# Attention with the next image's projections woven into the current image, keys times tokens instead of keys times values, and a mix phase that works in pairs

## What is computed

```
q, k, v = split(x @ W_qkv.T)                 # 8 heads of 32 channels
q = sigmoid(q);  k = sigmoid(k);  v = v / (scale * c // H)
sink_incoming   = 1 / (((q + EPS) * (k_sum + EPS)).sum(-1) + EPS)
source_outgoing = 1 / (((k + EPS) * (q_sum + EPS)).sum(-1) + EPS)
conserved_sink   = ((q + EPS) * ((k * source_outgoing).sum(2) + EPS)).sum(-1) + EPS
conserved_source = ((k + EPS) * ((q * sink_incoming).sum(2) + EPS)).sum(-1) + EPS
kv = einsum('bhnd,bhne->bhde', k, v * softmax(clip(conserved_source)) * n)
x_update = einsum('bhnd,bhde->bhne', q, kv) * sink_incoming * sigmoid(conserved_sink)
out = x_update @ W_proj.T + b_proj
```

## Time and profile before

| | |
|---|---|
| time, median of 3 runs | 5708.57 us (5692.53 to 5710.28) |
| the profiled execution | 5696.53 us, its span 5694.8 us |
| PE busy | 5394.3 us, 95% of the span |
| DVE, ACT, POOL busy | 3966.5, 2635.7, 2496.2 us |
| mix phase | from 2960 to 4055 us |
| attention phase | from 4055 to 5237 us |
| mean granted clock of TensorE over the execution | 0.973 of 2.4 GHz |

### The profile page before, as it was taken

One profiled execution on the slowest core, in us unless ns is written; L12 is line 12 of the kernel. 1 busy time (PEld: TensorE's weight loads), 2 busy tenths in 40 slices (PEclk: granted clock), 3 DMA queues, 4 the chain that ended last, 5 costly groups with the idle time before them and its releaser, 6 DMA issues. The chain is left out here.

```text
span 5694.8 us, 94139 instructions
## 1 busy us (share of the span) xinstructions
PE 5394.3 (95%) x28244; PEld 3773.4 (66%) x28244; DVE 3966.5 (70%) x6165; ACT 2635.7 (46%) x4948; POOL 2496.2 (44%) x1385
## 2 busy tenths in 40 slices
PE   8999779997999999999989999999899999997999
PEld 5666545554555555555547777777677777775999
DVE  5555656665999999999976666666455555555787
ACT  4444148775444333444335555555533333332555
POOL 0000034443999999999975445544111111110332
PEclk9999989998999999999999999999899999998999
DMA  1111668886444444444455555555322222222443
GB/s 43 45 45 39 167 176 241 245 242 191 152 149 149 150 151 147 152 149 148 150 148 174 174 182 178 176 185 174 129 89 91 89 92 89 88 95 74 119 122 113
DMA packets 357605, 784.70 MB, mean 138 GB/s; under 512 B 44223, under 2 KB 148339, under 8 KB 347946
## 3 DMA queue, kind: packets, MB, share of 16 engines
q1 hardware_dynamic: 342144, 731.51, 43.2%
q10 hardware_dynamic: 15344, 51.50, 2.3%
HBM read 448.08 MB, written 334.80 MB: 137 GB/s over the span
## 5 line engine op out<-in xcount | busy, mean ns | idle before, releaser
L717 POOL TENSOR_TENSOR co_prod<-co_cross 111x512 f32<-111x512 f32 x448 | 850.4, 1898 | 0.0
L651 ACT ACTIVATE co_y_out<-co_y_ps 112x512 f32<-112x512 f32 x448 | 268.0, 598 | 927.5 <-PE co_y_ps L597 922.7
L714 POOL TENSOR_TENSOR co_prod<-co_direct 111x512 f32<-111x512 f32 x448 | 577.3, 1289 | 201.5 <-PE co_y_ps L597 115.1
L691 DVE TENSOR_TENSOR co_direct<-co_v_ps,co_spec 111x1024 f32<-111x1024 f32 x448 | 543.7, 1214 | 91.8 <-PE co_v_ps L135 87.6
L1865 POOL TENSOR_TENSOR at_t<-at_t,at_p_bias 112x1024 f32<-112x1024 f32 x56 | 133.8, 2389 | 1030.9 <-DMA at_t<-t_tiles 1030.9
L693 DVE TENSOR_TENSOR co_cross<-co_v_ps,co_spec 111x1024 f32<-111x1024 f32 x448 | 541.9, 1210 | 0.0
L135 PE MATMUL co_v_ps<-co_v_high,co_col_fwd_high 112*111 112x512 f32 x896 | 506.1, 565 | 1.5 <-DVE co_cross L693 1.4
L595 PE MATMUL co_y_ps<-co_prod,co_col_inv 111*112 111x512 f32 x896 | 458.2, 592 | 0.0
L597 PE MATMUL co_y_ps<-co_prod,co_col_inv 111*112 111x512 f32 x896 | 457.5, 592 | 0.1
L671 DVE TENSOR_TENSOR co_v_low<-co_v_in,co_v_high 112x1024 fp32r<-112x1024 f32 x224 | 372.6, 1663 | 0.2
L135 PE MATMUL co_v_ps<-co_v_low,co_col_fwd_high 112*111 112x512 f32 x896 | 354.3, 395 | 0.0
(11 more groups left out here) (270 smaller groups left out, 14838.2 us busy)
## 6 DMA issues: line engine op xcount, KB each, us to landing
v_rows<-pr_rows_out SPq DMA_DIRECT2D x56, 1792.0 KB
co_v_in<-v_rows SPq DMA_DIRECT2D x448, 224.0 KB
y_rows<-co_y_out SPq DMA_DIRECT2D x448, 224.0 KB
mx_y_in<-y_rows SPq DMA_DIRECT2D x224, 448.0 KB, 3.7
at_n_raw<-n_t SPq DMA_DIRECT2D x112, 448.0 KB, 3.3
kern_rows<-kr_rows_out SPq DMA_DIRECT2D x28, 896.0 KB
st_x_in<-x SPq DMA_DIRECT2D x56, 448.0 KB, 10.6
pr_x_in<-x SPq DMA_DIRECT2D x112, 224.0 KB
```

Source lines behind the costliest of these rows:

```text
L651: nc.scalar.activation(y_out[:, b, :], y_ps[b % 2][:2 * SIDE, :], ACT.Copy).then_inc(y_ready, 1)
L691: nc.vector.tensor_tensor(direct[b % 2][:], v_ps[b % 2][:POINTS, :], spec[i][:, :2 * WIDE], ALU.mult).then_inc(real_terms, 1)
L714: nc.gpsimd.tensor_tensor(prod[b % 2][:, :WIDE], direct[b % 2][:, :WIDE], direct[b % 2][:, WIDE:], ALU.subtract).then_inc(real_ready, 1)
L717: nc.gpsimd.tensor_tensor(prod[b % 2][:, WIDE:], cross[b % 2][:, :WIDE], cross[b % 2][:, WIDE:], ALU.add).then_inc(combined, 1)
```

## The change

**Mix.** The two `inverse_rows` of tiles 0 and 1 are issued one behind the other, and those of tiles 2 and 3; `output_mm` moves ahead of `turn_gated`, directly behind `gate_mm`; DVE's order follows. ACT starts one more DMA per chunk, which stores the normalised tokens untransposed (`store_n1`, 448 KB, into `n1_tok`).

**Attention.** There are two `qk_t`, one for each of two images, and the 28 units of the next image are written between the steps of the current one; only the first image's stand by themselves. No value tiles are made. Instead keys are transposed 112 tokens at a time (`turn_keys`), scaled by the softmax weights straight out of PSUM (`scale_keys` on DVE), and multiplied with the untransposed tokens into a 256 x 256 matrix (`add_gram`, two fp32 products of 256 columns per 112 tokens); once an image the value weights `w_v` are applied to that (4 products). The split tokens are made once an image. The loop over images is written out in Python, so the code of all 8 images stands in the program. `t1` has 3 buffers instead of 4.

```diff
                     if before:
+                        output_mm(*before, 2)
                         turn_gated(*before, 3)
-                        output_mm(*before, 2)
...
                         inverse_rows(*now, 0)
+                        inverse_rows(*now, 1)
                         gate_mm(*now, 3)
-                        turn_gated(*now, 0)
                     if before:
                         output_mm(*before, 3)
+                    if now:
+                        turn_gated(*now, 0)
...
                     if now:
-                        inverse_rows(*now, 1)
                         if after:
                             gate_mm(*after, 0)
+                        output_mm(*now, 0)
                         turn_gated(*now, 1)
-                        output_mm(*now, 0)
...
+                def store_n1(s, u):
+                    g = s * 2 + u
+                    done(act, n1_ready, g)
+                    act.dma_start(d["n1_tok"][g], n1[u][:]).then_inc(n1_stored[u], 16)
...
+                    def turn_keys(n):
+                        if n >= 2:
+                            pe.wait_ge(key_scaled, b * NT + n - 1)
+                        for h in range(HALVES):
+                            last = nc.tensor.transpose(key_ps[n % 2][:TILE, h * 128:(h + 1) * 128],
+                                                       qk[:, 2 + h, n * TILE:(n + 1) * TILE], ident[:])
+                        last.then_inc(key_mm, 1)
+
+                    def add_gram(n):
+                        j, t = divmod(n, TILES)
+                        if t == 0:
+                            pe.wait_ge(tok_loaded[j % 2], (b * TOK_USES[j % 2] + j // 2 + 1) * 16)
+                        pe.wait_ge(key_scaled, b * NT + n + 1)
+                        for h in range(HALVES):
+                            last = nc.tensor.matmul(gram_ps[h][:, :CH], n_tok[j % 2][:, t, h * 128:(h + 1) * 128],
+                                                    keys[n % KEYS][:], start=n == 0, stop=n == NT - 1)
+                        last.then_inc(gram_mm, 1)
...
+                    units(0)
+                    pe.wait_ge(t2_ready, b * SUMS)
+                    pe.wait_ge(upd_ready, b * UPDS)
+                    wait_link(pe, im, "sel")
+                    head_sums(total_eps, flow_ps, flow_mm)
+                    units(1, 2, 3)
+                    wait_link(pe, im, "inv_low")
+                    for piece in range(PIECES):
+                        j, pair = divmod(piece, 2)
+                        pe.wait_ge(sum_ready, b * UNITS + max((j - 1) * BLOCKS + 2 * pair + 2, 0))
+                        spread_rows(wide_ps, j, range(2 * pair, 2 * pair + 2)).then_inc(spread_mm, 1)
+                        units(*range(4 + piece * 10 // PIECES, 4 + (piece + 1) * 10 // PIECES))
+                    units(14)
+                    wait_link(pe, im, "sel2")
+                    head_sums(total2_eps, kept_ps, kept_mm)
+                    units(15, 16, 17)
+                    pe.wait_ge(source_ready, b + 1)
...
+                    turn_keys(0)
+                    turn_keys(1)
+                    units(18)
+                    for n in range(NT):
+                        add_gram(n)
+                        if n + 2 < NT:
+                            turn_keys(n + 2)
+                        if n == TILES:
+                            units(19)
+                    units(20)
+                    pe.wait_ge(gram_ready, b + 1)
...
+                        if j < 6:
+                            units(22 + j)
...
+                    sigmoids(12, 13, 14, 15)
+                    wait_link(act, im, "clipped")
+                    nc.scalar.activation(source[:], clipped[:], ACT.Exp, accum_out=z_part[:]).then_inc(source_ready, 1)
...
+                    sigmoids(16, 17)
+                    nc.scalar.activation(alloc[:], kept[:], ACT.Sigmoid).then_inc(alloc_ready, 1)
...
+                    def scale_keys(n):
+
+                        j, t = divmod(n, TILES)
+                        dve.wait_ge(key_mm, b * NT + n + 1)
+                        at_least(dve, gram_mm, b * NT + n - KEYS + 1)
...
+                        nc.vector.tensor_tensor(keys[n % KEYS][:].rearrange(heads, x=2, c=HEAD),
+                                                key_ps[n % 2][:TILE, :CH].rearrange(heads, x=2, c=HEAD), each, ALU.mult
+                                                ).then_inc(key_scaled, 1)
```

More of the change, by code:

```diff
@@ L1912, in head_sums, with back, units @@
+                def back(im, front, beyond):
+                    b, qk, ahead = im.b, qk_t[im.odd], im.after()
+                    def units(*which):
+                        for u in which if front else ():
+                            unit(ahead, u)
                     def head_sums(sums, out_bank, done):
@@ L2015, in image @@
                         output(j - 1)
+                        if j < 6:
+                            units(22 + j)
                     output(CHUNKS - 1)
-                over_images(pe, image)
+                for u in range(UNITS):
+                    unit(Image(0, 0), u)
+                over_images(pe, back)
             @block.scalar
@@ new lines, in sigmoid, with back, sigmoids, next_high @@
+                def sigmoid(im, u):
+                    j, x = divmod(u, BLOCKS)
+                    act.wait_ge(qt_mm, im.b * UNITS + u + 1)
+                    nc.scalar.activation(qk_t[im.odd][:, x, j * CHUNK:(j + 1) * CHUNK], qt_ps[u % 2][:, :CHUNK], ACT.Sigmoid,
+                                         accum_out=part[im.odd][:, x, j:j + 1]).then_inc(qt_ready, 1)
+                def back(im, front, beyond):
+                    b, ahead = im.b, im.after()
+                    def sigmoids(*which):
+                        for u in which if front else ():
+                            sigmoid(ahead, u)
+                    def next_high(i):
+                        if front:
+                            high_part(ahead, i)
@@ L2210, in image @@
                         take_update(j)
-                        if more and j in (2, 3):
-                            low_part(b + 1, j - 2)
+                        if beyond and j == 4:
+                            low_part(ahead.after(), 0)
                         if j:
@@ L2216, in image @@
                     add_residual(CHUNKS - 1)
+                    if beyond:
+                        low_part(ahead.after(), 1)
                     measure(CHUNKS - 1)
-                over_images(dve, image)
+                first = Image(0, 0)
+                for i in range(CHUNKS):
+                    low_part(first, i)
+                low_part(first.after(), 0)
+                low_part(first.after(), 1)
+                over_images(dve, back)
 def ffn_phase(nc, d):
```

468 lines of the change are left out of this document (230 added, 238 removed).

## The result

The changed kernel takes **5608.09 us** (median of 4 runs, 5605.04 to 5614.06) against 5708.1 of the kernel before (4 runs); the ratio is 0.9832, with a 95% interval of 0.982 to 0.9843. Forecast were 5612 and a range of 5562 to 5662. The profiled execution has a span of 5612.2 us, 82.6 less than the one of before.

What follows compares the result with a forecast made beforehand. TensorE's own stream was taken to bound the mix phase, its stream and waits the attention. 5696.5 less 58 (attention) and 28 (mix) gave 5610.5 for a profiled-like execution, taken as 5612 us; range 5562 to 5662.

Steps and rivals of the forecast that it cites:

- TensorE's stream in an image: Attention: TensorE's full-clock work per image falls from 126 to about 120 us, summed as 120.4.
- The waits: Attention: TensorE's remaining waits sum to 10.7 us an image, little below the 11 of before.
- Products: Attention, key-token products: low parts and factors between VectorE's scalings make TensorE wait 0.6 + 0.6 + 1.4 us an image.
- Weighted sums: Attention: VectorE needs 20.6 us an image, under TensorE's 22.6, so no wait.
- The inverse: Attention: 5.2 us from const to low rows, under units 1 to 3 (3.6), leaves TensorE a 1.6 us wait.
- The clock's loss: Attention: half-clock time costs 3.7 us an image, half of before's, bounded by nothing and 7.
- rival (a): One gain fails: mix saves nothing (5640), or attention waits stay longer, 140 to 142 per image (5650 to 5660); chance 0.22.
- The last image: End of attention: without units covered waits are bare, so 116 us against 106, 5 of it half clock.
- Mix: Mix phase: four blocks of rows products become two, saving 0.5 us a chunk, -28 us in 56 chunks; bounds -5 and -50.
- the serial step: Attention's key step pays scaling and two hops each time, 0.5 to 0.7 us: 5725 to 5770; rival (b), chance 0.06.
- (c): Rival: the mix phase's first low part is late by 0.2 to 0.4 us a tile, 5685 to 5700; chance 0.06.
- That straight code costs nothing: Attention's image loop written out: no visible cost; by the skill, 7 boundaries would give back some 2 us each.

Runs made afterwards that it cites:

- The kernel with the three repairs: Changed kernel with GpSimd's bias additions later, unit 18 behind the second key-token product, new image's total and selection ahead of old one's last measure: 5535.85 us, ratio 0.9701.
- the kernels that took them away: Changed kernel with new image's total and selection ahead of old one's last measure, 5569.58 us; changed kernel with unit 18 behind the second key-token product, 5594.21 us.
- The kernel with one step of lead: Changed kernel with key transposes issued one step ahead of the products with tokens instead of two: 5811.12 us, ratio 1.018.
- the later biases: Changed kernel with GpSimd beginning an image's bias additions only behind the seventh weighted sum: 5585.29 us, ratio 0.9788.
- the fillers: Kernel with the three repairs, plus products nobody reads in TensorE's waits of the last image: 5525.19 us, ratio 0.9681.
- The pairs alone: Kernel before with the mix phase's rows products paired, but gate, turned gates and output in the old order: 5684.45 us, ratio 0.9961.

## Why the prediction was right, step by step

The time came out within 4 us, partly by luck. Errors cancelled: in the profiled executions the mix phase gave 9 us more than forecast and the seven images 6 more, the last image 8 less, and the 11.3 us ahead of the mix phase belong to no term.

- **TensorE's stream in an image** was 120.4 us by the sum. The window has 123.35 us busy at clock 0.95. The kernel with the three repairs does the same 4754 matmuls in 119.9 us busy an image at clock 0.99, so at full clock the work is about 118.7 (an estimate: 119.9 less 0.01 of 124). The error is in the new products, steps of 1.09 instead of 1.16, 2 us an image; by the price of 0.46 the 56 of them would be 25.8, not 25.5.
- **The waits**, 10.7 by the sum, are 11 in the image shown, but with other parts. Image start 2.5 for 2.7 and unit 18 1.9 for 2.1: right, and both confirmed by the kernels that took them away. Exponential 0.26 for 1.2. Products 0.3 for 2.6: this was an error of reasoning. When VectorE makes a low part between two scalings, the transposes are still a whole step ahead, and the delay comes out of that lead; I had deducted only the slack of one step. The kernel with one step of lead shows what the lead is worth. Weighted sums 0.8 (5.9 by 7) for nothing: VectorE was priced by the 0.62 us that one sum is busy, but they follow each other at 0.74, 28 x 0.12 = 3.3 us more. The inverse 4.6 (38.4 less 6.1, by 7) for 1.6: here **the step that failed is the duration of the high and the low part, taken from the image of the earlier trace rows**. 0.39 and 0.63 were right for a place where GpSimd was idle. The change moved the loads of the residuals to the front of SP's list, GpSimd's additions followed them under the inverse, and I had not laid GpSimd beside VectorE there. The Trainium skill ("SBUF — State Buffer", section "SBUF: two separate sides") says that VectorE and GpSimd share one pair of ports as an exclusive lock, held for a whole instruction, and that a VectorE copy in its fast mode or an operation with two inputs from SBUF asks for it. The rows agree in each point that they can show: the copy and the two-input subtraction wait out an addition of 2.39 us, the one-input reciprocal stays at 2.95.
- **The clock's loss** was put at 3.7, half of before's 7. By the window's mean, 0.10 of 134 us at half speed, it is at most 6.7; by busy time it is 123.35 less 118.7, 4.7. The places are the ones behind the waits. It was within the bounds given. The argument beside it misread a row: the wait of 3.0 at `const` is VectorE's for TensorE, not one of TensorE's; TensorE's longest in an image of before was the one for the exponential, 3.1. And the sign that was given for the clock, 0.97 in the attention, did not come: it was 0.93, which was to speak for rival (a), while the totals were 133.9 apart and spoke against it.
- **The last image**: forecast +10, measured +17.8. The forecast's 116 runs to the phase's end, with a tail of 2.5, so it is about 113.5 to the last residual sum, where 121.5 were measured: 8 us over. Three terms were mis-sized. The weighted sums at 0.62 instead of 0.74 are 3.3 us. GpSimd's additions under the inverse are 3.5 (121.5 to 118.0 with the later biases; the wait alone fell by 1.0, and the clock rose from 0.82 to 0.84). Half clock, 5 us by the sum, was worth at least the 6.7 that the fillers took off.
- **Mix**: -28 forecast, -37 measured, inside the bounds. A merged block saves 0.32, not 0.23. And the step "the transposes moved behind outputs give back or take some 0.1" missed what that move is for: it gives nothing by itself and keeps the pairs from waiting, which is worth 19 us (-38.1 against -17.5 and -1.3).
- **Rivals**: the serial step is real in price, 0.54 us, and slower than before by 1.8% when it occurs; the second step of lead kept it away. The late first low part in the mix phase, (c), did not come: waits for it are 3.5 us in the whole phase. The store costs nothing that the runs can show. That straight code costs nothing is not quite so. In the looped images of before the weighted sums follow each other at 0.67 us, and in its eighth image, written out, at 0.74, as in all images of after. That is 2 us of VectorE's time an image; the 2.10 at the loop's boundary are gone. No kernel here put the loop back, and why the steps differ is open.

```profile
4573.02 0.62 DVE L2136 SCALAR_TENSOR_TENSOR at_scratch<-at_bank_ps,at_qk_t 128x448 f32<-128x448 f32 x1
...
4573.68 0.62 DVE L2136 SCALAR_TENSOR_TENSOR at_scratch<-at_bank_ps,at_qk_t 128x448 f32<-128x448 f32 x1
...
5149.49 0.62 DVE L2136 SCALAR_TENSOR_TENSOR at_scratch<-at_bank_ps,at_qk_t 128x448 f32<-128x448 f32 x1
...
5150.22 0.62 DVE L2136 SCALAR_TENSOR_TENSOR at_scratch<-at_bank_ps,at_qk_t 128x448 f32<-128x448 f32 x1
```

By the rule of the Trainium skill ("TensorE: Matmul & The Clock Gate", Part 3 on packing small matmuls) that weight loads overlap running matmuls only when their row group differs, as the prediction quoted it, pairing would have been worth nothing. The pairs alone gave 17.5 us, and PEld was busy 786 us beside TensorE's 1080 of 1095; the measurement decides against it. The prediction left out that the same part also names a load into the background weight buffer as one that goes ahead of running matmuls, so these rows do not contradict the part as a whole.

## What to carry to other kernels

Work that is woven into waits pays twice: the wait is filled, and TensorE keeps its clock behind it; here the weaving was worth 158 us, while the same arithmetic with nothing in the waits was slower than the kernel before. When a change moves loads, follow them to the engine that they release: a GpSimd addition that cost nothing where it stood blocked VectorE for 3.0 us an image at its new place, and when it was moved by accident, it blocked the next instruction. And test the parts of a reordering apart and together: a part that gives nothing alone (the output ahead) can be what lets the other give all it has.

## What the runs showed of the hardware that I had not expected

VectorE's copy of 128 x 448 elements took 0.39 us, or up to 2.56 while GpSimd added; its two-input subtraction 0.63 or 2.64. In the image where the subtraction had begun 0.11 us ahead of the addition it took 0.63 again, and the addition 2.77 instead of 2.38: there the one that started first had its way. The weighted sums, which read one operand from PSUM, stayed at 0.62 beside the same additions.

In a last image with TensorE busy 138 of 175 us, in steps each behind a wait of half a microsecond, the clock stood at 0.62; with useless products in the waits of a last image that stood at 0.84, it stood at 1.00 and the image was 6% shorter.
